# Attention scores from keys and queries in two 11-bit parts, with projections placed one by one between the scores

## What is computed

```python
x = x + layernorm(attn(layernorm(x)))       # 16 heads of 16 dims, over all 1024 tokens
x = x + layernorm(ffn(layernorm(x)))        # shared gated FFN; 512 rows also go through one of 8 experts
# attn: zn = layernorm(z) * scale + bias; q, k, v = zn @ w_qkv
#       att = softmax(q @ k.T / 4); out = z + (att @ v) @ w_proj + b_proj
```

## Time and profile before

| | |
|---|---|
| runs | 992.9, 995.28, 995.99 us (median 995.28) |
| profiled execution | 993.8 us, of it 992.0 span |
| busy PE / DVE / ACT / POOL | 927.3 / 798.6 / 617.0 / 352.1 us |
| granted TensorE clock, mean | 0.968 |
| DVE row maxima (L1324) | 634.6 us, 1024 of them |
| PE: scores, values, max products | 275.2, 273.6, 246.4 us |

### The profile page before, as it was taken

One profiled execution on the slowest core, in us unless ns is written; L12 is line 12 of the kernel. 1 busy time (PEld: TensorE's weight loads), 2 busy tenths in 40 slices (PEclk: granted clock), 3 DMA queues, 4 the chain that ended last, 5 costly groups with the idle time before them and its releaser, 6 DMA issues.

```text
span 992.0 us, 16504 instructions
## 1 busy us (share of the span) xinstructions
PE 927.3 (93%) x6202; PEld 373.5 (38%) x6204; DVE 798.6 (81%) x1568; ACT 617.0 (62%) x720; POOL 352.1 (35%) x473
## 2 busy tenths in 40 slices
PE   5879999999999999999999999999999989957985
PEld 3323332323343344333343343332422423136763
DVE  4688879898979878889889979889799798265765
ACT  3116778777867777777767767777676777801110
POOL 3052003004635253229733623258243232822113
PEclk9778999999999999999999999999999999988998
DMA  4924120620260305300631033104430000240001
GB/s 135 155 32 64 47 55 12 98 61 8 75 109 24 97 13 77 75 13 22 113 110 60 8 54 80 36 8 104 91 99 13 12 13 20 95 170 22 1 0 64
DMA packets 60544, 58.14 MB, mean 59 GB/s; under 512 B 19136, under 2 KB 49680, under 8 KB 60080
## 3 DMA queue, kind: packets, MB, share of 16 engines
q1 hardware_dynamic: 59840, 55.83, 25.6%
q0 software_dynamic: 384, 1.05, 0.3%
q10 hardware_dynamic: 240, 0.20, 0.2%
HBM read 18.06 MB, written 9.17 MB: 27 GB/s over the span
## 4 chain that ended last, share of the span: by engine, by line
PE 79%; DVE 9%; ACT 3%; issue 3%; DMA 2%; POOL 2%; SPq 1%; ACTq 0%; POOLq 0%; DVEq 0%
PE obank L1061 22%; PE sc L1047 19%; PE ring L1028 16%; PE ring L946 9%; PE ring L953 4%; DVE mx L1324 4%; PE sc L1178 3%; PE ring L938 2%; DVE st L1253 2%; ACT prob L870 1%; PE sc L953 1%; DMA x_sb<-x 1%; DMA qp<-parts 1%; PE ring L1071 1%; ACT zT L773 0%
## 5 line engine op out<-in xcount | busy, mean ns | idle before, releaser
L1324 DVE TENSOR_REDUCE mx<-ring 128x1 f32<-128x512 f32 x1024 | 634.6, 681 | 107.9 <-PE ring L1028 106.9
L870 ACT ACTIVATE prob<-sc 128x1024 f32<-128x1024 f32 x512 | 495.8, 1021 | 132.6 <-PE sc L1047 131.4
L1047 PE MATMUL sc<-qp,kp 48*128 48x512 bf16 (+1 forms) x2048 | 275.2, 380 | 2.2 <-DMA qp<-mp 0.9
L1061 PE MATMUL obank<-prob,vaug 128*32 128x512 f32 x2048 | 273.6, 606 | 0.7 <-ACT prob L870 0.7
L1028 PE MATMUL ring<-kp,qp 48*128 48x512 bf16 x1024 | 246.4, 392 | 17.0 <-DVE mx L1324 13.0
L1028 PEld LDWEIGHTS ring<-kp,qp 48*128 48x128 bf16 x1024 | 75.0, 93 | 296.4 <-DVE mx L1324 228.5
L1047 PEld LDWEIGHTS sc<-qp,kp 48*128 48x128 bf16 (+1 forms) x2048 | 98.9, 95 | 106.8 <-ACT prob L870 25.2
L626 POOL TENSOR_TENSOR hid<-hid,b 128x512 f32<-128x512 f32 x24 | 30.3, 1271 | 110.9 <-ACT hid L831 110.9
L1061 PEld LDWEIGHTS obank<-prob,vaug 128*32 128x32 f32 x2048 | 40.3, 108 | 66.1 <-issue 63.9
L640 POOL TENSOR_TENSOR resid<-qkf,parts 128x1024 f32<-128x1024 f32 x11 | 23.4, 2131 | 114.4 <-ACT parts L807 114.4
L634 POOL TENSOR_TENSOR yA<-yA,sums 128x512 f32<-128x512 f32 x15 | 19.0, 1269 | 110.4 <-DMA sums<-reciprocal_scratch 110.4
(11 more groups left out here) (212 smaller groups left out, 797.9 us busy)
## 6 DMA issues: line engine op xcount, KB each, us to landing
kp<-parts SPq DMA_DIRECT2D x96, 128.0 KB, 4.9
qp<-parts SPq DMA_DIRECT2D x189, 64.0 KB, 2.9
x_sb<-x SPq DMA_DIRECT2D x7, 1024.0 KB, 6.1
out<-hid SPq DMA_DIRECT2D x4, 1024.0 KB, 5.3
yA<-oT SPq DMA_DIRECT2D x124, 32.0 KB
sums<-reciprocal_scratch SPq DMA_DIRECT2D x31, 128.0 KB
x_scratch<-x SPq DMA_DIRECT2D x3, 1024.0 KB, 4.5
qp<-mp SPq DMA_DIRECT2D x128, 2.0 KB
```

Of the source, the lines that this page charges most:

```text
L870: nc.scalar.activation(prob[:, e % 2, 2 * a:2 * a + 2, :].rearrange("p g n -> p (g n)"), sbuf2[a][:, :], ACT.Exp, scale=0.25).then_inc(s_f ...
L1047: ins = nc.tensor.matmul(dst[:, j * HALF:(j + 1) * HALF], kp[rows, h, kt * P:(kt + 1) * P], qp[rows, qh, h, :], start=plane == 0, stop=pla ...
L1061: ins = nc.tensor.matmul(obank[i * VW:(i + 1) * VW, :], vaug[:, b % 2, kt, c0:c0 + VW], prob[:, v % 2, i, :], start=(kt == 0), stop=(kt == ...
L1324: nc.vector.tensor_reduce(mx[:, u % 2, n:n + 1], src[:, :], AX.X, ALU.max).then_inc(rv_free, 1)
```

## The change

Keys and queries are scaled by a power of two (from a bound computed at the start out of the weights and the layer norm scale), and split into two fp16 parts. Four products of parts then suffice: three of 16 dims, and the smallest one with 14 of 16, which with the two rows of the maxima makes 64 rows. One matmul makes a head's score.

```diff
+KS = HD - 2
+KM = KR + KS + 2
-PRODUCTS = [(0, 0), (1, 0), (0, 1), (2, 0), (1, 1), (0, 2)]
+PRODUCTS = [(0, 0), (1, 0), (0, 1), (1, 1)]
-QK_AT = (2, 2, 4, 4)
-Z_AT = ((18, 18, 20, 20), (9, 9, 17, 17))
-V_AT = (25, 25, 49, 49)
-P_AT = (19, 19, 21, 21)
-QK_NEXT_AT = (33, 33, 35, 35)
-X_AT = (41, 41, 42, 42)
-H_AT = (44, 44, 47, 47)
-U_AT = (57, 57)
-W_AT = (59, 59, 61, 61)
+QK_AT = (1, 2, 4, 5)
+Z_AT = ((17, 19, 21, 23), (9, 11, 13, 15))
+V_AT = (26, 28, 30, 31)
+P_AT = (17, 19, 22, 24)
+QK_NEXT_AT = (33, 35, 37, 39)
+X_AT = (41, 42, 43, 44)
+H_AT = (45, 47, 48, 50)
+U_AT = (57, 58)
+W_AT = (59, 60, 61, 62)
-Y_STATS = (21, 21, 25, 25)
-X_STATS = (33, 35)
+Y_STATS = (20, 21, 25, 26)
+X_STATS = (34, 35)
-                    for plane in range(2):
-                        h = plane_of(g * GH + 2 * a, plane)
-                        for j in range(2):
-                            rows = slice(64 * j, 64 * j + (KM if plane else KR))
-                            ins = nc.tensor.matmul(dst[:, j * HALF:(j + 1) * HALF], kp[rows, h, kt * P:(kt + 1) * P],
-                                                   qp[rows, qh, h, :], start=plane == 0, stop=plane == 1)
+                    h = g * GH // 2 + a
+                    for j in range(2):
+                        rows = slice(64 * j, 64 * j + KM)
+                        ins = nc.tensor.matmul(dst[:, j * HALF:(j + 1) * HALF], kp[rows, h, kt * P:(kt + 1) * P],
+                                               qp[rows, qh, h, :], start=True, stop=True)
-                if 1 <= w < B and tau in (47, 49):
+                if 1 <= w < B and tau in (50, 53):
+            for a, w in enumerate((wk, wq)):
+                for k in range(KD):
+                    for r in range(2):
+                        nc.scalar.activation(wsq[:, a, k, r, :], w[:, k, :], ACT.Square, scale=lnp[:, r, k:k + 1])\
+                            .then_inc(s_wsq, 1)
+            def second_part(b, c):
+                n = 2 * KD * b + c
+                pool.wait_ge(s_part, 2 * n + 2)
+                nc.gpsimd.tensor_tensor(parts[:, c % 2, 1, :], qkf[:, :], parts[:, c % 2, 0, :], ALU.subtract)\
                     .then_inc(s_second, 1)
```

More of the change, by code:

```diff
@@ L198, in build @@
         nm = sb("nm", [P, 2, GH * QT])
-        mp = sb("mp", [GH * QT, 2, 2, P], bf16)
+        mp = sb("mp", [GH * QT, 2, 2, P], f16)
+        wmax, wroot, power, scale, unscale = (sb(n, [P, 2]) for n in ("wmax", "wroot", "power", "scale", "unscale"))
         st6 = [sb(f"st6{i}", [P, NT, 6]) for i in range(2)]
@@ L241, in build @@
         mout = resid[:, 0:D]
-        fixed = resid[0:2, 0:HALF].bitcast(bf16)
+        fixed = resid[0:2, 0:HALF].bitcast(f16)
+        wsq = hid[:, 0:4, :].rearrange("p t d -> p (t d)").bitcast(bf16).rearrange("p (a k r d) -> p a k r d", a=2, k=KD, r=2)
+        ones = act[:, 0, 0:P // 2].bitcast(bf16)
         sbuf2 = [ctx.enter_context(nc.psum_tensor(f"sc{i}", [P, 2 * HALF], f32)) for i in range(2)]
@@ L361, in build @@
         PACK = [16 * len(STACK), 16 * len(STACK) * NH]
-        LARGEST = [item for item in STACK if item[1] == 0]
-        REST = [item for item in STACK if item[1] > 0]
+        LARGEST = [item for item in STACK if item[1] == HD]
+        REST = [item for item in STACK if item[1] < HD]
         K0 = Q0 = 16 * len(LARGEST)
@@ L696, in _ @@
                         add("p", w - 1, i)
-                if 1 <= w < B and tau == 25:
+                if 1 <= w < B and tau == 27:
                     mean_of("y", w - 1, 0, D)
@@ L703, in _ @@
                     nc.gpsimd.tensor_tensor(x1[:, :, :], x1[:, :, :], x_sb[:, :, :], ALU.add).then_inc(s_x1, 1)
-                if w + 1 < B and tau == 35:
-                    split(w + 1, 0)
+                if w + 1 < B and tau == 36:
+                    second_part(w + 1, 0)
                 if 1 <= w < B and tau == 36:
@@ L720, in _ @@
                         add("w", w - 1, i)
-                if 1 <= w < B and tau == 50:
+                if 1 <= w < B and tau == 54:
                     mean_of("u", w - 1, 0, F)
@@ L804, in ring_item @@
                             sc.wait_ge(s_q0, Q0)
-                    nc.scalar.activation(qkf[:, half], src[:, :], ACT.Copy).then_inc(taken, 1)
+                    nc.scalar.activation(qkf[:, half], src[:, :], ACT.Identity, scale=scale[:, c % 2:c % 2 + 1]).then_inc(taken, 1)
                     sc.wait_ge(taken, count)
@@ L866, in _ @@
                     if 0 <= e < NS:
+                        if e == 0 and a == 0:
+                            sc.wait_ge(s_power, 4)
                         if e >= 2 and a == 0:
@@ L877, in _ @@
                     nc.scalar.activation(oT[:, u % 2, :], obank[:, :], ACT.Copy).then_inc(s_oT, 1)
-                if 1 <= w < B and tau in (46, 48):
-                    i = int(tau == 48)
+                if 1 <= w < B and tau in (49, 52):
+                    i = int(tau == 52)
                     sc.wait_ge(s_added["h"], 4 * (w - 1) + 2 * i + 2)
@@ L1003, in _ @@
             pe.wait_ge(s_first, C_FIRST)
+            pe.wait_ge(s_ones, 1)
+            for a in range(2):
+                for i in range(2 * KD):
+                    pe.wait_ge(s_wsq, 2 * KD * a + i + 1)
+                    ins = nc.tensor.matmul(sbuf2[0][:, a * D:(a + 1) * D], ones, wsq[:, a, i // 2, i % 2, :], start=(i == 0),
+                                           stop=(i == 2 * KD - 1))
+                ins.then_inc(s_bound, 1)
             for key in RING_AT[-1]:
@@ L1025, in max_products @@
                         h, qt, kh = max_item(t, j)
[L1026 removed]
+                        rows, h = slice(64 * (h % 2), 64 * (h % 2) + KR), (g * GH + h) // 2
                         dst = open_r("max", t, j)
```

149 lines of the change are left out of this document (72 added, 77 removed).

## The result

The changed kernel takes **1016.5 us** (median of 4 runs, 1014.1 to 1019.2), the kernel before 994.9 beside it (992.9 to 996.0): a ratio of 1.022, 95% interval 1.019 to 1.025. The prediction was 1011, from 990 to 1020. The profiled execution spans 1014.1 us against 992.0, with nearly the same mean granted clock (0.966 against 0.968).

What follows compares the result with a forecast made beforehand. Slots were taken as 2.49 us, bound by the loop over DVE's first maximum and the value product, plus max(items, other DVE work). Main part +20.8 and ends -5 gave +15.8 on 993.8: 1009.6, or 1011 on the median's side, range 990 to 1020.

Steps and rivals of the forecast that it cites:

- The bound: Slots without items: a 2.48 us loop over DVE's first maximum and PE's value product, with score matmuls beside it.
- The rival in which the saved time reaches the items: PE before an item: getting ahead by 0.43 us a slot opens 60 large items less; 980 us, chance 14%.
- Items one by one: Items issued singly instead of in pairs: 1.92 us per large item; +1.9 a window (1, 2), four `w` +0.4.
- Lost cover: DVE's other work in slots without enough items beside it: +7.8 us in window 1, +8.6 in window 2.
- the cover isn't needed: Rival: moved DVE work may cost less than its length if m1 and m2 run on; 995 us, chance 12%.
- slot 53: Tau 53 of a window, gate and `u` statistics without an item: +2.9 us, a slot of 5.4 us.
- the tanh's wait of 1 us: Upper bound on cover: the gate at tau 50 and 53 also waits 1 us for its tanh.
- Window 3's terms: Large items +1.1, `f` statistics +0.8, `y` +1.1, late `p` item -0.8, `w`, transposes -0.4: taken as +2 us.
- The transposes' 1.5: Single `z`, `x`, `u` transposes lose the wait of pairs filling all three banks: 1.5 us gained a window.
- The ends: Start -0.7, first slots with scores at half clock -2.3, scores behind the last max product -2: together -5 us.
- The clock rival: PE's 0.6 us pause in each slot lets the clock fall to half in a tenth of slots: 1042 us, 6%.
- a clock under 1.0 between 120 and 860 us: One of the signs that would show the prediction wrong, read from the granted clock.

Runs made afterwards that it cites:

- kernel with doubled scores: The changed kernel with each score matmul issued twice into the same place: 1025.1 us, ratio 1.031.
- the product alone: The changed kernel with every item, statistic, gate and POOL step back in the slots of the kernel before, short score product kept: 983.8 us, ratio 0.989.
- the one with the old product and new places too: The kernel before, eight score matmuls a slot, with items one by one in the changed kernel's slots and one residual moved to POOL: 1024.9 us, ratio 1.031.
- The kernel with the early value product: The changed kernel with the value product ahead of the third and fourth max product instead of behind them: 1075.7 us, ratio 1.082.
- the kernel with the later value product: The changed kernel with the old placement, value product one slot later between second and third max product, scores last: 1079.3 us, ratio 1.086.
- the kernel with the earlier tanh: The changed kernel with D_AT's second entry at slot 52 and ScalarE's second tanh at slot 51 instead of 52: 1012.3 us, ratio 1.018.
- the kernel with the earlier copy: The kernel with the later value product, with ScalarE's copy of the value bank ahead of its slot's exponentials instead of behind: 1004.4 us, ratio 1.011.

## Why the prediction was right, and where it was off

**The bound** was read rightly. PE's 93% did not make it the bound; slots stay at 2.49, the wait of the weight load before the fourth max product is 0.60 (predicted about 0.6), and 105 us of PE work taken away or put back move the time by 9 to 11 us. The rival in which the saved time reaches the items falls by the 1.92 us behind a single item and by the kernel with doubled scores.

**Items one by one** cost what the sum says (1.92 large, 1.06 `w`). An `mt` beside a single large item stays hidden: slot 33 lasts 4.40.

**Lost cover** was the right main term, and the rival "the cover isn't needed" falls: putting most of it back gains 19.5 us. The term that was mis-sized is slot 53. The sum had +2.9 there; with the two slots behind it, window 2 shows 6.33 + 3.77 + 2.56 - 3 x 2.49 = +5.2. The prediction had the tanh's wait of 1 us only as an upper bound, and the clock only as a rival for the whole run. With the tanh moved, the slot is 5.27 and window 1 217.7. This one place is 2.3 us over its term in windows 1 and 2, more than the 1.8 that each window is over its forecast, and window 3 has it too. (Window 3's terms as written add up to +2.2, and were taken as +2.)

**The transposes' 1.5** came, but the reason given was half of it at most: single items save 0.6 to 0.8 a window with the old product, the shorter scores alone 1.9 to 2.1, and both together 1.3 to 1.6. That is one part of why the product alone is worth 11 us and not the 5 that the sum had as ends.

**The ends**: window 0 gained 2.8 where 1.5 was forecast, the scores behind the last maximum 1.3 where 2 was. Of window 0's gain 1.6 us lie in slot 6, which has no scores: 5.00 before, 3.41 in every other kernel, the one with the old product and new places too. Before's half clock lasted 17.1 us there, the others' 10.2 or 13.7. So the scores gave less than the 2.8. The start can't be judged to a few tenths: the first maximum falls between 32.3 and 33.8 us in profiled executions of kernels with the new product, whose starts are alike. Nor can the rest, forecast at 0 and 1.5 longer: in the same executions it takes 120.7 to 124.6 us.

**The clock rival** (1042) did not come as such: with the load's wait of 0.60 us in each slot the granted clock stays 1.00 (415 to 620 us above, 205 us in a row). PE's matmul records show only 0.13 us of idleness there. The kernel with the early value product is the stronger test: PE idles 0.57 us in plain slots by its records, and from 230 to 430 us the clock is 1.00 too. What the Trainium skill tells in "TensorE: Matmul & The Clock Gate", section "A second HAM failure mode: psum-queue depth-cycling", of a kernel whose clock swings with its pauses is not what such slots do here. Longer pauses do bring falls, though: nearly all of the 20 in the kernel with the later value product stand behind pauses of 1.81 us. And one of the prediction's own signs of being wrong, a clock under 1.0 between 120 and 860 us, was met three times, behind the pauses of slot 53.

All in all the mechanisms hold, and the forecast was 5.5 us low on 1016.5. The largest error behind it is slot 53 and the clock behind it in three windows. Part of the closeness is luck: the sum is 20.8 for the places less 5 for the product, where the experiments show 30.1 to 32.7 for the places and 11.0 for the product. Both are too small, by 9 to 12 and by 6 us, and the two errors stand against each other. The best kernel found is the new product with the old places: 983.8, 1.1% below before.

## What to carry to other kernels

Look for the loop before counting busy time: an engine at 93% can have work that lies beside the loop, and cutting that work only makes its wait longer. Side work of two engines costs the larger of the two when it stands in one slot and the sum when it is spread, so here spreading items evenly lost 32.7 us. When an order is changed, go through every bank's loop and every engine's own queue at the new place: both large misses here (the early value product, the late copy) and the tanh of slot 53 were waits that no row of the old order showed.

## What the runs showed of the hardware that was not expected

- An exponential over 128x1024 elements takes 1112 ns with its scale from a column in SBUF and 1021 ns with a number. For the copy of 128x512 out of the ring to `qkf`, an Identity with a scale from a column in the changed kernel and a Copy without one before, it is 687 against 595. That is 91 ns and 92 ns an instruction, at both lengths.
- The granted clock fell to half in the middle of a stretch at full clock, for 3.4 us up to 13.7 us, behind one pause of PE of a few microseconds: 4.0 and 4.2 us in the changed kernel, 1.5 us (window 3) and 3.1 us in the kernel with the product alone. In the kernel with the earlier tanh, three pauses of 2.9 us were followed by a fall, none, and a fall. Before's one pause of 2.7 us, at 798 us, was followed by none, the three of 2.4 us in the kernel with the early value product each by one. In the kernel with the later value product PE paused 26 times for 1.81 us before the last maximum; 18 of these pauses were followed by a fall within 3 us, 8 were not, among them the one before 290.00. The length of a pause alone does not decide. Two falls (at 274.6 us there, at 728.1 us in the kernel with the earlier copy) stand behind pauses of only 0.78 and 0.70 us. Where slots with and without a fall can be compared, one fall of 3.4 us costs 1.1 us.
